# A graph layer and a routed feed-forward on one Trainium2 core: the layer's second product moved one step later and computed feature-major for 512 tokens at once

## The reference

```python
x = x + gnn(layernorm(x), adj)
x = x + ffn(layernorm(x))

# gnn: eps, W1 128x512, b1, rms weight, W2 512x128, b2
agg = eps * x + adj @ x
h = silu(rmsnorm(agg @ W1 + b1) * rms_weight)
out = h @ W2 + b2

# ffn: 8 experts, the best 2 of each token
xn = layernorm(x) * gamma + beta
logits = xn @ Wr + br
w_full = softmax over the two largest logits, 0 elsewhere
y = sum_e (gelu(xn @ W1[e] + b1[e]) @ W2[e] + b2[e]) * w_full[..., e]
```

## Time and profile before

| | |
|---|---|
| median of 3 runs | 435.77 us (435.37 to 436.22) |
| the profiled execution | 438.06 us, its span 436.2 us |
| PE busy | 399.6 us, 92% |
| DVE, ACT, POOL busy | 295.7, 281.3, 300.2 us |
| granted PE clock, mean | 0.990 |

### The profile page before, as it was taken

How to read it: one execution, slowest core, us unless ns; L and a number is a source line. 1 busy time by engine, 2 the same in 40 slices (tenths; PEclk the granted TensorE clock), 3 DMA queues, 4 the chain that set the end, 5 groups by cost and what they waited for, 6 DMA issues and landing times.

```text
span 436.2 us, 11992 instructions
## 1 busy us (share of the span) xinstructions
PE 399.6 (92%) x2932; PEld 346.7 (79%) x2932; DVE 295.7 (68%) x1276; ACT 281.3 (64%) x652; POOL 300.2 (69%) x439
## 2 busy tenths in 40 slices
PE   1899999999999999999979997799977999999994
PEld 1467877876778777777869886799877999999994
DVE  5596877888887889876762552356665666856553
ACT  1377776787677788777786543468665777545441
POOL 1233558877778788887887778656756666887774
PEclk9999999999999999999999999799999999999999
DMA  7777873233322331111154333544445543433311
GB/s 230 234 226 271 290 230 88 75 112 109 112 77 83 112 110 45 44 51 51 51 145 127 102 93 101 144 128 131 132 135 142 145 122 106 113 112 107 106 38 38
DMA packets 41031, 53.11 MB, mean 122 GB/s; under 512 B 5826, under 2 KB 35778, under 8 KB 40324
## 3 DMA queue, kind: packets, MB, share of 16 engines
q1 hardware_dynamic: 32896, 32.54, 27.1%
q0 software_dynamic: 6096, 18.52, 12.2%
q10 hardware_dynamic: 1972, 1.28, 1.0%
HBM read 37.61 MB, written 22.31 MB: 137 GB/s over the span
## 4 chain that ended last, share of the span: by engine, by line
PE 69%; DVE 10%; issue 7%; SPq 6%; ACT 2%; another core or an unknown queue 2%; DMA 1%; POOL 1%; DVEq 1%; ACTq 0%; POOLq 0%
PE banks L811 13%; PE banks L794 12%; PE banks L628 11%; PE banks L651 11%; PE banks L616 7%; PE banks L637 5%; PE banks L673 3%; PE banks L774 2%; SPq L425 2%; PE banks L663 2%; SPq L414 1%; SPq L421 1%; SPq L424 1%; DVE result L1551 1%
## 5 line engine op out<-in xcount | busy, mean ns | idle before, releaser
L558 POOL DMA_INDIRECT out<-result,rows_in x92 | 89.2, 970 | 54.2 <-DVE result L1551 41.5
L811 PE MATMUL banks<-w_sb,hidden_e 128*128 (+1 forms) x736 | 102.9, 282 | 0.2 <-issue 0.2
L811 PEld LDWEIGHTS banks<-w_sb,hidden_e 128*128 128x128 f32 x736 | 92.6, 195 | 0.9 <-issue 0.5
L949 ACT ACTIVATE hidden_e<-banks 128x512 f32<-128x512 f32 x92 | 54.9, 597 | 47.1 <-PE banks L794 32.4
L502 POOL DMA_INDIRECT rows_dram<-rows_out,row_of x64 | 67.4, 1053 | 14.0 <-issue 10.5
L628 PE MATMUL banks<-gw_sb,agg 128*128 128x512 f32 x128 | 67.3, 611 | 0.9 <-DVE gw_sb L994 0.9
L651 PE MATMUL banks<-gw_sb,hidden_t 128*128 128x128 f32 x512 | 67.6, 275 | 0.0
L651 PEld LDWEIGHTS banks<-gw_sb,hidden_t 128*128 128x128 f32 x512 | 63.5, 192 | 0.8
L859 ACT ACTIVATE hidden<-banks 128x512 f32<-128x512 f32 x64 | 38.2, 597 | 30.8 <-PE banks L628 27.6
L637 PEld LDWEIGHTS banks<-fixed,hidden 128*128 128x128 f32 x256 | 30.5, 141 | 34.4 <-issue 29.7
L942 ACT ACTIVATE xg_t<-banks,ones 128x128 f32<-128x128 f32 x92 | 33.5, 364 | 30.5 <-PE banks L774 20.4
(11 more groups left out here) (150 smaller groups left out, 763.1 us busy)
## 6 DMA issues: line engine op xcount, KB each, us to landing
rows_in<-rows_dram SPq DMA_DIRECT2D x92, 132.5 KB
adj<-adj_t SPq DMA_DIRECT2D x16, 512.0 KB, 4.4
x_tok<-x SPq DMA_DIRECT2D x16, 256.0 KB, 3.4
rows_dram<-idle_in POOLq DMA_DIRECT2D x1, 3710.0 KB
rows_dram<-idle_in SPq DMA_DIRECT2D x28, 132.5 KB
out<-result,rows_in POOLq DMA_INDIRECT x92
w_sb<-w SPq DMA_DIRECT2D x1, 1024.0 KB, 6.1
b_bc<-b SPq DMA_DIRECT2D x1, 1024.0 KB, 10.6
```

The lines of the kernel that those rows point to most:

```text
L558: nc.gpsimd.indirect_dma_start(out=out, out_offset=bass.IndirectOffsetOnAxis(ap=rows_in[:, i % RING][:, IDX_AT:IDX_AT + 1].bitcast(U32), a ...
L811: last = pe.matmul(y_ps(i)[:, w], hidden_e[:, i % 4, w * HCE + c], w2_sb[:, bass.ds(at + c * D, D)], start=(c == 0 and i >= EARLY), stop=( ...
L949: nc.scalar.activation(hidden_e[:, i % 4], h_ps(i), ACT.Gelu).then_inc(gelu_done, 1)
```

## The change

The second product is taken out of the step in which the hidden rows are transposed. It runs in the next step, for a whole group: four products of 512 columns whose stationary operand is the weight, so that features are on partitions. The bias and the input are added there by one DVE operation from a transposed copy of the input, which SP loads (16 loads of 256 KB that did not exist before); the bias product L648 and its preparation are gone. One product for each tile (136 columns: identity and router weights side by side) then turns the rows back and gives the raw logits; `keep_x2` copies both to the output rows. DVE multiplies the logits by 1/deviation, a new first step of `route`, which has 13 steps now. `turn_to_features`, `expert_input` and `router` are gone. `normalise2` runs a step later than before (group s-5), and the orders of DVE, POOL and of `tail` are rewritten to fit.

```diff
@@ POOL
             def scale2(g):
...
+                    pool.wait_ge(route_link, ROUTE * (g - 2) + 1)
...
             def send_rows(g, t):
...
+                    pool.wait_ge(xn2_ready, g + 1)
...
+            shares(a)
             send(NG - 3, 0, 1)
             place_high(2)
             scale2(z)
...
-            shares(a)
-            send(None, 0, 8)
...
+            place_high(8)
+            send(None, 0, 9)
+            shares(z)
@@ PE
+            def narrow(g):
+
+                if g >= 1:
+                    pe.wait_ge(x2_ready, g)
+                else:
+                    pe.wait_ge(consts_in, CONSTS)
+                pe.wait_ge(hidt_copied, TPG * (g + 1))
                 for c in range(HC1):
-                    last = pe.matmul(z_ps[:, t * P:(t + 1) * P], hidden_t[:, g % 2, c, t * P:(t + 1) * P], gw2_sb[:, c],
-                                     start=False, stop=True, skip_group_check=True)
-                if t == TPG - 1:
-                    last.then_inc(z_done, 1)
...
+                    last = pe.matmul(z_ps, gw2_sb[:, c], hidden_t[:, g % 2, c], start=(c == 0), stop=(c == HC1 - 1))
+                last.then_inc(z_done, 1)
+
+            def turn_back(g):
+
+                pe.wait_ge(x2_ready, g + 1)
...
                 for t in range(TPG):
...
+                    last = pe.matmul(back_ps[:, t // 2, t % 2], x2_t[:, g % 2, t * P:(t + 1) * P], turn_by[:],
+                                     start=True, stop=True)
+                last.then_inc(back_done, 1)
...
                 if g2 is not None:
                     widen(g2, 0)
+                if g4 is not None:
+                    narrow(g4)
                 if g1 is not None:
                     aggregate(g1)
...
-                if s - FOLD_AT in range(FOLDS):
-                    sum_expert_weights(s - FOLD_AT)
                 if g3 is not None:
                     turn_hidden(g3, 0)
                 if g2 is not None:
                     widen(g2, 1)
                 if g3 is not None:
                     turn_hidden(g3, 1)
-                    narrow(g3, 0)
+                if g4 is not None:
+                    turn_back(g4)
...
@@ PE, tail and the place ahead of the tiles
-                if at == (0, 1):
-                    router(NG - 2)
-                elif at == (6, 1):
-                    turn_to_features(NG - 1)
-                elif at == (6, 2):
+                if at == (2, 1):
+                    turn_back(NG - 1)
+                elif at == (4, 2):
                     rank_pairs(NG - 2)
-                elif at == (7, 1):
-                    router(NG - 1)
-                elif at == (11, 1):
+                elif at == (9, 2):
                     rank_pairs(NG - 1)
-                elif at == (15, 2):
+                elif at == (14, 2):
                     turn_columns(1)
...
             pe.wait_ge(weighted, NT)
+            narrow(NG - 1)
@@ ACT
+            def keep_x2(g):
+                act.wait_ge(back_done, g + 1)
...
+                nc.scalar.activation(rows_out[:, g % RO, :, X2_AT:X2_AT + BACK].rearrange("p (b u) k -> p b u k", u=2),
+                                     back_ps, ACT.Copy).then_inc(x2_kept, 1)
...
                 if g4 is not None:
-                    normalise2(g4, (0, 1))
+                    keep_x2(g4)
+                if g5 is not None:
+                    normalise2(g5, (0, 1))
...
-                if g4 is not None:
-                    expert_input(g4)
@@ DVE
+                nc.vector.scalar_tensor_tensor(x2_t[:, g % 2], z_ps, gb2_col[:, 0:1], x_d[:, g % XD], ALU.add, ALU.add
+                                               ).then_inc(x2_ready, 1)
```

420 lines of the change are left out of this document (198 added, 222 removed).

## The result

The changed kernel takes 453.49 us (median of 4 runs, 451.71 to 455.15), the kernel before 435.72 in its runs beside them (435.37 to 436.22): ratio 1.0406, 95% interval 1.0359 to 1.0454. The profiled execution took 455.15 us with a span of 453.3.

The account below looks back on a forecast made before the run. PE was taken to bound the group phase, PE and ACT then taking turns; +6.0 and -0.6 there, +2.9 to the first tile, -4.0 in the first tiles gave +4.3 on 435.8: 440.1 us, range 437 to 446, wide range 430 to 449.

Parts of the forecast that it names:

- The premise that the table's columns set the start of the late loads: Handover to tile phase: SP waits for the table's first row, so the late loads and the kernel's end move with it.
- PE's own work: PE in the group phase: net 0.80 us less a step, 11.86 us instead of 12.66, if PE never waited.
- The loop that the move closes: PE and ACT take turns through narrow and aggregate in the group phase: step 13.38 us, 0.72 more than before.
- The expert steps: Group-phase steps 7 to 10, with the expert product: 13.92 us against 13.69, 0.23 more in each.
- Steps 3 and 4: Group-phase steps lacking normalise2 or keep_x2: loop at 11.74 us or less, counted as -0.6 for them.
- The handover, +2.9: Last aggregate to first tile: 35.1 us against 32.25, +2.9, with 6.66 + 3.44 for the last step.
- The first tiles, -4.0: First tile to the table's columns: one step less -2.2, tail -1.2, ranks -0.6; sum -4.0, bounds -5 to -1.
- I count them as even: POOL's 1 to 3 us of waits in the first tiles, set against the earlier kernel's own waits there.
- The distance to the end, "unchanged": From SP's first late load to the last instruction: unchanged at 172 us.
- Rival 1: PE stays the bound in the group phase: 16 x -0.80 = -12.8, tail -4.0, 419 us; chance 0.11.
- Rival 3: narrow at widen's price (5.8), or DVE delays ranks and POOL tiles 1, 4 by 3 us: 446 to 449; chance 0.10.

Follow-up runs that it names:

- norm_late: Changed kernel with both pairs of normalise2 on ACT moved behind the fourth keep_turned, out of the burst: step 12.92 us, ratio 1.0266.
- rank_late: Changed kernel with the ranks on PE placed behind the fourth transposes instead of ahead of them: step 13.43 us, ratio 1.0348.
- narrow_behind: Changed kernel with narrow on PE placed behind aggregate and the first transposes instead of ahead of them: step 12.86 us, ratio 1.0343.
- eps_fold_late: Changed kernel with DVE's second expert operation and add_epsilon moved behind choose: expert step 13.72 us, ratio 1.0368.
- cols_early: Changed kernel with the first table's columns turned on PE at the start of the last group's step, not in its middle: ratio 1.0354.
- handover: Changed kernel with the edits of rank_late, cols_early and pool_tail, plus one send moved ahead of scale2(z) on POOL: ratio 1.0218.
- after_again: The changed kernel run once more with no edit: ratio 1.0403.
- combo_best: Changed kernel with all loop and handover edits, late normalise2 pairs put back between copies, columns turned behind the second product in the last step: ratio 1.0076.
- pool_tail: Changed kernel with shares(a) on POOL behind the weight copies for tiles 1 and 2, and the last group's scatters sent earlier: ratio 1.0396.

## Why the prediction was right or wrong

The sign and the mechanism of the loop were right, the size was not: 440.1 was forecast, the wide range ended at 449, and the kernel took 453.5. What failed are terms of the sum: the last step of the handover (6.66 us and a `narrow` of 3.44, measured 8.47 and 5.78), POOL's waits in the first tiles, which were counted as even with what they replace, the expert steps, and steps 3 and 4. The premise that the table's columns set the start of the late loads failed too.

**PE's own work**: right. `turn_back` takes 149.69 - 148.76 = 0.93 us (0.95), `narrow` 158.48 - 154.97 = 3.51 (3.44). The Trainium skill (Perfetto Trace Analysis, Transposes) would have the turn done by a transpose; the trace shows where that rule stops here: the product that turns and gives the logits costs 0.93, the transposes and the router together cost 1.31.

**The loop that the move closes**: right to 0.06 us (13.44 for 13.38, `narrow` at t = 8.20 for 8.22), borne out by `norm_late`, `rank_late` and `narrow_behind`. Two things in it were off. PE's wait was to be named after ACT's copy at the fourth transposes; it is named after `choose`. DVE's chain, which I had costed at nothing, ends later than the 5.8 I gave it: the ranks start at 152.83, t = 6.06, and the fourth transposes right behind them at t = 6.38, where I had 6.34.

**The expert steps**: mis-sized. I gave them 13.92, from PE and ACT alone; the first takes 13.72 and the three behind it 14.29, because DVE has two expert operations ahead of `choose` there, and the step behind them takes 13.58. DVE of the changed kernel in such a step:

```profile
89.75 0.65 DVE L1026 SCALAR_TENSOR_TENSOR b_bc<-b_bc,banks 128x512 f32<-128x512 f32 x1
...
93.25 0.75 DVE L1030 SCALAR_TENSOR_TENSOR w_sb<-w_sb,gamma_col,b_bc 128x512 f32<-128x512 f32 x1
...
96.71 0.28 DVE L1176 TENSOR_TENSOR chosen<-fixed,key 128x112 bf16<-128x112 f32 x1
```

`eps_fold_late`, which moves the second of them and `add_epsilon` behind `choose`, shows it: with them moved all four take 13.72, so DVE adds 0.57 in three of them, and my 13.92 was 0.2 too long. Against the forecast the five steps are 1.1 us over (3 x 14.29 + 13.72 + 13.58 = 70.17 for 4 x 13.92 + 13.38 = 69.06). I had written that 0.5 us on this chain would start to count and did not look at which steps add it.

**Steps 3 and 4**: "-0.6" was wrong by 1.6. I took the loop as shorter there and did not ask how long these steps were before: 11.27 and 12.39 us; after they take 12.14 and 12.54, with waits of 0.41, 0.19 and 0.67 us at transposes for ACT's copies. No run tests them alone.

**The handover, +2.9**: mis-sized, +7.15, the largest miss. Two of its three steps came exactly: from the end of an `aggregate` or `narrow` to the next `narrow`, 208.72 - 200.52 and 220.43 - 212.23, 8.2 each. The last took 8.47 for 6.66 (the prediction does not list what the 6.66 is made of), and the last `narrow` held PE 5.78 us for 3.44. In `cols_early`, with the clock full, 0.9 us of the first and all of the second are gone; 0.6 of that 0.9 is the low clock in the products between the ranks and `narrow` (230.17 to 232.41 for 229.85 to 231.47). So some 2.9 us of the miss are the clock, for which the prediction has no term. About 0.9 of the 8.47 remains (0.6 in `handover`, where ACT waits 0.20 and 0.33 us in that burst for PE's second transposes and `turn_back`): the last burst is shorter by less than I subtracted.

**The first tiles, -4.0**: mis-sized, +0.84. The term that failed is "I count them as even": POOL's 1 to 3 us were there (1.83 + 1.09 = 2.9), and the ranks (0.45) and the columns (1.21) waited too. All waits of PE between the first tile and the columns come to 2.5 us before (0.55, 0.76, 0.40, 0.58, 0.20) and 6.5 after (those four and 0.55, 0.55, 0.83): 4.0 more, where the sum had 0.6 less. -4.0 + 4.0 + 0.6 = +0.6, near the +0.84 measured. With the order of POOL mended and the columns early the stretch is 31.9 in `handover` against the 31.5 of the forecast. So the -4.0 was there to be had, and the kernel as written did not have it. What it is worth is another matter: I took the columns for what the late loads wait for. In the changed kernel the first late load follows POOL's last scatter, by 3.4 us (275.37 to 278.74), and by 3.3 to 3.7 in every experiment; before, where the table came last, it was 5.5 (258.40 to 263.87). By the first late load the miss of this stretch is 3.6 us and not 4.8.

**The distance to the end, "unchanged"**: +2.2 from the first late load. `after_again` and the experiments put the stretch from the first fill anywhere from 168 to 175.6, so it is not shown that the change is its cause, nor that it is not; why it moves stays open. There is only one trace of the kernel before (171.4).

**Rival 1** (PE stays the bound, 419) is excluded, and no order that was tried reaches it: `combo_best` is still 0.8% slower than before. The Trainium skill (Perfetto Trace Analysis, Identifying the Most-Contended Engine) would have the engine of highest occupancy relieved first, and for PE looks at weight loads and at the arithmetic done, not at busy time. By busy time the trace names PE (128.82 of 130 us); by weight loads it does not (100.47, below DVE's 109.90). Relieving PE, to 117.97, came with a longer step. What decides here is the chain PE, ACT, PE, and no occupancy shows it. **Rival 3** (446 to 449) came nearest, with one part wrong: POOL held up tiles 1 and 4 by 2.9 us and DVE's chain delayed the ranks, as it said, but `narrow` at full clock never cost what a lone `widen` does.

## What to carry to other kernels

- Gathering the small products of a bound engine into one block saves its own time, but the small products were what it did while it waited for another engine's copies. Before moving them, follow the order of the waiting engines once around: if each of two engines has one instruction in front of which the whole other's turn must end, the step is the sum of the two turns. Here it gained 0.58 us a step to move the block behind what the other engine waits for (`narrow_behind`), and 0.52 to shorten the other's turn (`norm_late`).
- A wait's name is that of the first instruction in line that is late. Compute when the next one behind it could have started: removing 10.1 us of named waits moved the step by 0.01 us.
- Ask again, for the changed kernel, which of two conditions comes last. The late loads waited for the table before and for the last scatter after, and columns that were turned 1.3 us earlier (`after_again`) did not start them earlier.
- A chain "just beside" the bound must be worked out for the longest kind of step, not for the common one; and a hidden term with a known size (POOL's 1 to 3 us) is a term of the sum, not of the range, until a row shows what it replaces.

## What the runs showed of the hardware

PE's granted clock fell between the phases after waits that are short by themselves. Windows of the changed kernel, 220 to 240 us:

```profile
220.00:230.00 10.00, 6.32 (x30) 3.89 (x30) 6.23 (x39) 6.40 (x13) 6.66 (x12) 1.00 0.17 56
230.00:240.00 10.00, 7.96 (x21) 3.84 (x21) 3.55 (x22) 2.50 (x7) 3.83 (x6) 0.66 0.41 103
```

The same windows in `cols_early`:

```profile
220.00:230.00 10.00, 6.51 (x33) 4.03 (x34) 6.53 (x42) 6.18 (x13) 6.98 (x12) 1.00 0.25 72
230.00:240.00 10.00, 7.52 (x41) 4.76 (x39) 5.69 (x31) 5.67 (x13) 5.01 (x9) 1.00 0.44 122
```

In the first, `narrow` (232.41) held PE 5.78 us, against 3.5 at full clock, behind a wait of 2.63 us at the ranks and 0.78 at `narrow`; the granted clock of 0.66 means that a part of the stretch ran at 1.2 GHz. In `cols_early`, behind 2.32 and 0.78 us, it held 3.5 and the clock stayed at 2.4 GHz. The lengths of the waits do not settle it, since the same waits went both ways in other runs. `rank_late` and `handover` have 1.28 us at the fourth transposes and 1.00 at `narrow`; the first kept the clock (3.5 us), the second did not (5.06). Five runs with 2.63 and 0.78 have a last `narrow` of 5.2 to 6.5 us (changed twice, `norm_late`, `pool_tail`, `eps_fold_late`); the sixth, `narrow_behind`, has 3.5. Rows of `rank_late` and `narrow_behind`:

```profile
218.63 3.67 PE L658 MATMUL banks<-hidden_t,gw_sb 128*128 128x512 f32 x8 [1.00 <-ACT hidden_t L868]
229.99 3.67 PE L658 MATMUL banks<-hidden_t,gw_sb 128*128 128x512 f32 x8 [0.78 <-issue]
```

So 1.5 to 3 us hang here on something that these runs do not show, and it stays open whether `cols_early` kept the clock up or only met it so. The Trainium skill (TensorE: Matmul & The Clock Gate, HAM oscillation — how this bites in real kernels) describes a like pattern, waits between bursts after which the next burst starts at the low clock; its case waits for transfers, for 3 to 5 us, ours for VectorE and ScalarE, for 2.63 at most.
